# Layer norm 0 and the first projection of block 1 moved into the slots of attention layer 2

## The chip, the cores and the metric

The kernel runs on one core of one Trainium2 chip. The metric is the device time of one execution in microseconds (us): the median of three runs of the kernel before is 800.58 us (800.31 to 802.76). The engines are called by their short names: PE is TensorE (matmuls; PEld is its weight load), DVE is VectorE, ACT is ScalarE, POOL is GpSimd, and SP is SyncE, which here issues all DMAs.

## The reference

`x` is 2048 x 256, `adj` is a 2048 x 2048 matrix of zeros and ones, everything in float32. Four blocks follow one another, each with a residual and a layer norm:

```python
def _gat_layer(x, W, adj):                  # block 0: two such layers
    Wh, Ws = jnp.split(x @ W, 2, axis=-1)
    a = jax.nn.softmax(Wh @ Ws.T, axis=-1) * adj
    return jax.nn.leaky_relu(a @ Wh + x, 0.01)

x = layernorm(x + gat(gat(x)))                                          # layer norm 0
# block 1: A_ = adj + I, d = rsqrt(A_.sum(1))
x = layernorm(x + relu((A_ * d[:, None] * d[None, :]) @ x @ W))
# block 2
x = layernorm(x + relu(adj @ x / (adj.sum(1) + 1e-5) @ Wn.T + bn + x @ Ws.T + bs))
# block 3
x = layernorm(x + adj @ (relu(adj @ (x @ W1) + b1) @ W2) + b2)
```

## The kernel before

The rows are cut into 16 row tiles of 128 (`NT = 16`), and 2048 columns into 4 chunks of 512 (`NCH = 4`). A float32 product is made from high and low halves: `exact3` runs three matmuls for each 128 rows of the contraction (high by high, low by high, high by low). Every engine has its own program, written out by hand, and waits on semaphores; `ge(engine, signal, count)` is such a wait.

**Attention layers** (`layer`, l = 0 and 1, called layers 1 and 2 here). A layer first projects all rows, and then goes through 16 slots, one row tile each; `slot(b, u)` handles tile t = b + u. Slots 4 and on stand in a hardware loop. In its slot PE computes the four chunks of scores of tile t (`score`, 24 matmuls of 512 columns), transposes the masked probabilities of tile t-1 (`turn`, 16 transposes), and multiplies them with the values (`attend`, 32 matmuls). In layer 1 it also transposes the finished rows of tile t-2 (`rows`, line 1783), between score chunks 2 and 3. ACT runs the exponentials (`exp`), rounds the transposed probabilities (`hi`) and scales half of the sum (`lo_half`); DVE takes the maxima (`chunk_max`, `row_max`), the low halves (`lo`), the rest of the scaling (`scaled`) and `finish` to `finish5`: leaky relu, the residual, and mean and variance of the row, for tile t-2. POOL masks with the adjacency (`mask`), adds the layer's input (`residual`) and prepares the next query (`query`). SP loads adjacency rows and, in layer 2, input rows (`load`, lines 401 and 404).

**Layer norm 0 and the projection of block 1**, a stage of its own between layer 2 and block 1. For each of the 16 tiles: DVE normalises the rows (`n_rows`, line 1327) into one of four buffers `nrow`, SP stores them (`store0`, line 443, queue order t = 0 to 15), PE transposes them (line 1871) into one bank, ACT and DVE take high and low halves (`n_hi`, `n_lo`), PE projects them with `w1` (`n_proj`, six matmuls of 256 columns), ACT and DVE scale and split the result into `pm` (`n_moving`). The square roots of all variances are taken in two pieces (`n_deviation`, line 851), after the last exponential; the square root of the degrees (`dsq`, line 875) as well.

**Block 1** (the path taken with 0/1 adjacency is `exact`; `general` is the other one, and the choice is made by a flag that each engine reads into a register: `If(low > 0): general() Else: exact()`). SP reads each adjacency tile from HBM as bfloat16, transposed on the way (`turn_halves`, line 439; a ring of 4 buffers `at16`), POOL widens it into `adjr` (`widen`, line 664), and PE sums over it (`main_sum`, chunks c = 0 to 3, four matmuls of 512 columns each), then transposes the finished rows (`rows`, line 1944) and projects them for block 2 (`project`). The order on SP around the stage is:

```python
for t in range(RING):            # RING = 4; each waits for the end of all attention sums
    turn_halves(t)
...                              # store0 of tiles 0 to 15, then wait until all are stored
# in exact():
for t in range(RING, 2 * RING):
    turn_halves(t)
# then bout, bhid, and per slot: load_res (line 474), turn_halves(slot + 8)
```

`load_res` brings back the stored rows of a tile for the residual of block 1; DVE adds them (line 1468), takes statistics, and normalises (`xs`, line 1500), and PE needs that for `rows` (line 1944). The buffers `at16` and `adjr` lie over buffers of the attention layers, so that they can be filled only when those are done with.

Of the kernel before, what the change touches and what calls it, by code (L numbers as in the profile page):

```python
# [13 lines left out]
P = 128  # L14
# [45 lines left out]
def adjacency_resnet(nc, x, adj, w_gat, w_gcn, w_neigh, b_neigh, w_self, b_self, w1, b1, w2, b2, out):  # L60
# [26 lines left out]
    with ctx:  # L87
# [24 lines left out]
        nrow = xs + zb  # L112
# [14 lines left out]
        const = sb("constants", [P, 2])  # L127
        eps, one = const[:, 0:1], const[:, 1:2]
# [23 lines left out]
        xtall_l = sb("xtall_l", [P, KT, N], F32R, gat)  # L152
        wst_h = sb("wst_h", [P, KT, N], F32R, gat)
# [4 lines left out]
        wg_h = sb("wg_h", [P, KT, 2 * D], F32R, gat)  # L158
        wg_l = sb("wg_l", [P, KT, 2 * D], F32R, gat)
        arow16 = sb("arow16", [P, N], BF16, gat)  # L160
# [21 lines left out]
        quick = ExitStack()  # L182
        adjr = sb("adjr", [P, NT, N], F32R, quick)
        at16 = [sb(f"at16_{r}", [P, NT, P], BF16, quick) for r in range(RING)]
# [108 lines left out]
        s_dinv = sem("degree_inverses")  # L293
        s_sd0 = sem("norm0_deviation")
# [3 lines left out]
        n_out = [sem(f"norm0_rows_stored_{c}") for c in range(NCH)]  # L298
# [52 lines left out]
        def attention_bank(b, u):  # L351

            return jb[1] if isinstance(b, int) and b + u == NT - 1 else ob0

# [16 lines left out]
        def _(sp):  # L371
# [13 lines left out]
            for l, g in enumerate(G):  # L385
# [38 lines left out]
                store_halves(0, 0)  # L424
                with sp.Fori(1, NT // 2) as half:
                    b = 2 * half
                    store_halves(*before(b, 0))
                    load(b, 0)
                    store_halves(b, 0)
                    load(b, 1)  # L430
                store_halves(NT - 2, 1)

            def turn_halves(t):
                sp.wait_ge(s_a16, 16 * NT)
                if t < RING:
                    ge(sp, G[-1].av, 4 * NT)
# [4 lines left out]
            def store0(t, c):  # L441
                sp.wait_ge(n_new, t + 1)
                sp.dma_start(xs_rows[t], nrow[c][:, :]).then_inc(n_out[c], 16)

            for t in range(RING):
                turn_halves(t)
            with sp.Fori(0, NT // NCH) as q:
                for c in range(NCH):
                    store0(NCH * q + c, c)
            for c in range(NCH):  # L450
                sp.wait_ge(n_out[c], 16 * NT // NCH)
# [5 lines left out]
            def stages(quick):  # L457
                for k, a in enumerate(aggs):
# [37 lines left out]
                    def slot(b, u, fin=True):  # L496
# [9 lines left out]
                        if quick and a is C and b + u + 2 * RING < NT:  # L506
                            turn_halves(b + u + 2 * RING)
# [32 lines left out]
            def general():  # L540

                for r in range(RING):
                    sp.wait_ge(s_at[r], 16)
                for c in range(NCH):
                    load_nat(0, c)
# [5 lines left out]
            def exact():  # L551
                for t in range(RING, 2 * RING):
                    turn_halves(t)
# [10 lines left out]
        def _(pool):  # L564
# [7 lines left out]
            nc.gpsimd.tensor_tensor(bsum[:, :], bsum[:, :], bs_raw, ALU.add).then_inc(s_bsum, 1)  # L572

            for l, g in enumerate(G):
# [54 lines left out]
                slot(NT - 2, 1, nxt=False)  # L629
                slot(NT, 0, main=False, nxt=False)  # L630
# [25 lines left out]
            def widen(t):  # L656
                r = t % RING
                pool.wait_ge(s_at[r], 16 * (t // RING + 1))
                if t == 0:

                    ge(pool, G[-1].av, 4 * NT)
                    ge(pool, G[-1].msk, 4 * NT)
                    ge(pool, G[-1].zx, NT)
                nc.gpsimd.tensor_copy(adjr[:, t, :], at16[r][:, :, :].rearrange("p a i -> p (a i)"))\  # L664
                    .then_inc(s_conv, 1)

# [3 lines left out]
            def exact():  # L670
                for t in range(NT):
# [11 lines left out]
        def _(act):  # L683
# [22 lines left out]
            features(1)  # L706

            def layer(l, g, previous):
# [90 lines left out]
                def slot(b, u, main=True, av=True, fin=True, last=False):  # L799

                    p = before(b, u)
                    if av:
# [23 lines left out]
                slot(0, 0, av=False, fin=False)  # L826
                slot(0, 1, fin=False)
                slot(2, 0)
                slot(2, 1)
                with act.Fori(2, NT // 2 - 1) as half:  # L830
# [18 lines left out]
            def n_deviation(first, last):  # L849
                ge(act, G[-1].mv, last)  # L850
                nc.scalar.activation(sd[:, first:last], mv[:, first:last, 1], ACT.Sqrt, bias=eps[:, :])\
                    .then_inc(s_sd0, 1)

            def n_hi(t, u):
                act.wait_ge(n_xtr, t + 1)
                ge(act, n_prj, t - 1)
                copy(xt_h[u][:, :, :], xb[u][:, 0:D].rearrange("p (k i) -> p k i", k=KT)).then_inc(n_xth, 1)

            def n_moving(t, u):
                act.wait_ge(n_prj, t + 1)  # L860
                if not isinstance(t, int):
                    alone(act, passed["scalar"])
# [1250 lines left out]
```

## Time and profile before

| | |
|---|---|
| median of 3 runs | 800.58 us |
| profiled execution, its own time | 800.49 us |
| its span, first to last instruction | 798.7 us |
| mean granted TensorE clock | 0.977 of full speed |
| PE busy | 742.2 us (93%) |
| DVE, ACT, POOL busy | 466.6, 336.8, 322.9 us |

The span is cut into stretches by what runs in them: projections and layer 1 up to about 261 us, the projections of layer 2 to 293 us, its slots to 497 us, the stage of layer norm 0 to 530.5 us, the blocks after that. Some 1.8 us of the profiled time lie outside the span. A line of the timeline gives start, duration, engine, line of the kernel, operation, output and inputs; brackets give the idle time of the engine before it and what ended it.

### The profile page before, as it was taken

The page shows a single profiled execution, that of the slowest core. Times are in us where ns is not written, and L with a number is a line of the kernel's source. Part 1 is how long each engine was busy: PE and PEld are TensorE (multiplying, and loading weights), DVE is VectorE, ACT ScalarE, POOL GpSimd, SP SyncE. Part 2 cuts the span into 40 slices and gives each one's busy share as a digit, 9 for nine tenths or more (in the row PEclk, how much of TensorE's full clock was granted, in tenths as well). Part 3 has the DMA queues.
Part 4 walks back from the last instruction along what each step waited for, and adds up shares of the span by engine and source line. Part 5 has one row for each costly group of instructions (what it writes and reads, how often), then busy time and mean ns, then how long its engine had stood idle before and what let it go on. Part 6 is the DMA issues. An engine that isn't in the chain of part 4 may idle for free.

```text
span 798.7 us, 13828 instructions
## 1 busy us (share of the span) xinstructions
PE 742.2 (93%) x4122; PEld 630.4 (79%) x4122; DVE 466.6 (58%) x1054; ACT 336.8 (42%) x803; POOL 322.9 (40%) x313
## 2 busy tenths in 40 slices
PE   6979999999999989999999999466999999999996
PEld 5868888888888878888888888355888768879895
DVE  3667777767776555555464656443555655562377
ACT  4656565656555444343434445231222423331222
POOL 1047676766665225555546463305310011112222
PEclk9999999999999999999999999788999999998998
DMA  6052424242331303131322220669642222320033
GB/s 197 1 210 82 159 80 151 85 138 98 124 113 53 118 1 113 60 119 59 118 72 105 89 89 12 161 94 176 159 112 80 66 90 83 89 70 8 1 94 105
DMA packets 67747, 76.60 MB, mean 96 GB/s; under 512 B 36848, under 2 KB 61040, under 8 KB 63600
## 3 DMA queue, kind: packets, MB, share of 16 engines
q1 hardware_dynamic: 67696, 75.97, 31.3%
q8 instruction: 26, 0.43, 0.2%
q14 instruction: 25, 0.20, 0.1%
HBM read 48.69 MB, written 18.87 MB: 85 GB/s over the span
## 4 chain that ended last, share of the span: by engine, by line
PE 67%; issue 13%; DVE 7%; SPq 4%; DMA 3%; ACT 3%; POOL 2%; DVEq 0%; POOLq 0%; ACTq 0%
PE scores L1644 32%; PE ob L1644 25%; PE tb L1758 6%; SPq L439 3%; DMA rin<-self_term_scratch 2%; ACT stationary L685 1%; DVE stationary L1075 1%; POOL prob L594 1%; PE tb L1734 1%; PE xb L1783 1%; DVE xs L1500 1%; DVE xs L1208 1%; DMA keep<-in_x 1%; POOL zb L642 1%; POOL zb L640 1%
## 5 line engine op out<-in xcount | busy, mean ns | idle before, releaser
L594 POOL TENSOR_TENSOR prob<-prob,arow 128x512 f32<-128x512 f32 x128 | 193.2, 1530 | 169.2 <-ACT prob L770 169.2
L1644 PE MATMUL ob<-val,stationary 128*128 128x512 f32 x960 | 184.6, 344 | 0.0
L1644 PEld LDWEIGHTS ob<-val,stationary 128*128 128x128 f32 x960 | 146.7, 189 | 18.8
L1075 DVE TENSOR_TENSOR stationary<-tb,stationary 128x512 fp32r<-128x512 f32 x128 | 85.8, 689 | 70.7 <-ACT stationary L685 70.6
L685 ACT ACTIVATE stationary<-tb 128x512 fp32r<-128x512 f32 x128 | 73.0, 593 | 114.4 <-PE tb L1758 114.4
L1644 PE MATMUL ob<-pm,adjr 128*128 128x512 f32 (+1 forms) x512 | 109.5, 356 | 10.3 <-issue 5.4
L1644 PE MATMUL scores<-wst_h,whs_h 128*128 128x512 f32 x256 | 104.1, 407 | 3.8 <-ACT prob L770 3.8
L1644 PE MATMUL scores<-pm,adjr 128*128 128x512 f32 (+1 forms) x512 | 104.9, 345 | 0.0
L1644 PEld LDWEIGHTS ob<-pm,adjr 128*128 128x128 f32 x512 | 82.8, 199 | 23.0 <-issue 11.9
L1145 DVE TENSOR_REDUCE row_values<-scores 128x1 f32<-128x512 f32 x128 | 86.5, 688 | 24.4 <-PE scores L1644 24.3
L1644 PE MATMUL scores<-wst_h,whs_l 128*128 128x512 f32 x256 | 100.3, 392 | 0.0
L1644 PE MATMUL scores<-wst_l,whs_h 128*128 128x512 f32 x256 | 100.1, 391 | 0.0
L770 ACT ACTIVATE prob<-scores,row_values 128x512 f32<-128x512 f32 x128 | 86.6, 689 | 5.8 <-DVE row_values L1152 5.0
L1644 PEld LDWEIGHTS scores<-pm,adjr 128*128 128x128 f32 x512 | 79.8, 192 | 9.2
L1758 PE MATMUL tb<-ident,prob 128*128 128x128 f32 x512 | 72.2, 272 | 3.1 <-POOL prob L594 3.1
L1758 PEld LDWEIGHTS tb<-ident,prob 128*128 128x128 f32 x512 | 60.9, 140 | 13.1 <-POOL prob L594 3.9
L1644 PEld LDWEIGHTS scores<-wst_h,whs_h 128*128 128x128 f32 x256 | 48.2, 188 | 13.4 <-issue 4.5
L640 POOL TENSOR_TENSOR zb<-zb,rin 128x256 f32<-128x256 f32 x16 | 11.8, 737 | 111.5 <-DVE zb L1426 111.5
L1644 PEld LDWEIGHTS scores<-wst_h,whs_l 128*128 128x128 f32 x256 | 48.0, 188 | 10.5
L664 POOL CAST adjr<-at 128x2048 fp32r<-128x2048 bf16 x16 | 30.3, 1903 | 60.4 <-DMA at<-adjacency_halves 60.4
L1644 PEld LDWEIGHTS scores<-wst_l,whs_h 128*128 128x128 f32 x256 | 48.3, 189 | 7.5
L1185 DVE SCALAR_TENSOR_TENSOR arow<-arow 128x2048 bf16<-128x2048 f32 x16 | 43.7, 2731 | 5.0 <-issue 3.0
(160 smaller groups left out, 987.3 us busy)
## 6 DMA issues: line engine op xcount, KB each, us to landing
arow<-in_adj SPq DMA_DIRECT2D x32, 1024.0 KB, 5.2
adjacency_halves<-arow SPq DMA_DIRECT2D x16, 512.0 KB, 3.0
xres<-features_scratch SPq DMA_DIRECT2D x48, 128.0 KB, 2.1
features_scratch<-xs SPq DMA_DIRECT2D x40, 128.0 KB, 1.7
keep<-in_x SPq DMA_DIRECT2D x4, 512.0 KB, 7.0
xres<-in_x SPq DMA_DIRECT2D x16, 128.0 KB, 2.1
self_term_scratch<-rst SPq DMA_DIRECT2D x16, 128.0 KB, 1.7
rin<-self_term_scratch SPq DMA_DIRECT2D x16, 128.0 KB, 2.1
```

Of the source, the lines that this page charges most:

```text
L439: sp.dma_start_transpose(at16[t % RING][:, :, :], a16_rows[t]).then_inc(s_at[t % RING], 16)
L594: nc.gpsimd.tensor_tensor(prob[u][:, cs], prob[u][:, cs], arow[u][:, cs], ALU.mult).then_inc(g.msk.sem, 1)
L640: nc.gpsimd.tensor_tensor(zb[u][:, :], zb[u][:, :], rin[u][:, :], ALU.add).then_inc(a.rb.sem, 1)
L642: nc.gpsimd.tensor_tensor(zb[u][:, 0:HID], zb[u][:, 0:HID], bhid[:, :], ALU.add).then_inc(a.rb.sem, 1)
L664: nc.gpsimd.tensor_copy(adjr[:, t, :], at16[r][:, :, :].rearrange("p a i -> p (a i)"))\
L685: return nc.scalar.activation(dst, src, ACT.Copy, **kw)
L770: nc.scalar.activation(prob[u][:, cs], scores[:, cs], ACT.Exp, bias=nmax[u][:, :], accum_out=rs[u][:, c:c + 1]).then_inc(g.ex.sem, 1)
L1075: return nc.vector.tensor_tensor(dst, v, h.bitcast(F32), ALU.subtract)
L1145: nc.vector.reduce_max(mx[u][:, c:c + 1], scores[:, c * CH:(c + 1) * CH], AX.X)\
L1185: nc.vector.scalar_tensor_tensor(arow16[:, :], arow[u][:, :], 1.0, arow16[:, :], ALU.mult, ALU.not_equal, accum_out=bits[:, bass.ds(t, 1)])\
L1644: return nc.tensor.matmul(o, l, r, start=start, stop=stop)
L1758: last = nc.tensor.transpose(tb[c % 2][:, q * P:(q + 1) * P], prob[u][:, j * P:(j + 1) * P], ident[:, :])
```

## The change

What it does:

- `n_rows`, `n_hi`, `n_lo`, `n_proj`, `n_moving` of tiles 0 to 11 run inside slots 4 to 15 of layer 2 (slot t handles tile t-4), those of tiles 12 to 14 among the last attention sums, tile 15's after them. Only the two `xs` buffers are used. One bank, `xb0`, takes the transposes and the projection (halves of it); the last four tiles alternate with a second one.
- `n_deviation` runs for two tiles at the end of each odd slot of layer 2 on ACT, ahead of `lo_half`, and is followed by an exponential of a constant (`spent`), which brings the exponential's table back.
- `dsq`, `rdeg`, `dinv` are computed at the start of layer 2's slots.
- In both layers PE's `rows` comes after score chunk 3, no longer before it, and DVE's `rows_lo` after `row_max`.
- SP issues `turn_halves` 0 to 2 early in layer 2, 3 after its scores, and only 4 and 5 in `exact()` (before: 0 to 3 after the attention, 4 to 7 in `exact()`). `store0(t)` follows `load(t + 4)` in the loop.
- POOL widens tiles 0 and 1 before the last `residual`, 2 and on after the branch.
- PE computes tiles 0 and 1 of block 1 side by side, chunk by chunk, with tile 15's `n_rows` and `n_proj` among them.
- On PE the condition is turned round: `If(low < 1): exact() Else: general()`.

```diff
-        nrow = xs + zb
 # sync
+            load(2, 0)
+            for t in range(RING - 1):
+                turn_halves(t)
+            load(2, 1)
+            with sp.Fori(2, NT // 2) as half:
+                b = 2 * half
+                for u in range(2):
+                    load(b, u)
+                    store0(b + u - 4, u)
+            turn_halves(RING - 1)
+            for t in range(NT - 4, NT):
+                store0(t, t % 2)
...
             def exact():
-                for t in range(RING, 2 * RING):
+                for t in range(RING, RING + 2):
                     turn_halves(t)
 # gpsimd
                 slot(NT - 2, 1, nxt=False)
+                if l == LAYERS - 1:
+                    widen(0)
+                    widen(1)
                 slot(NT, 0, main=False, nxt=False)
...
             def exact():
-                for t in range(NT):
+                for t in range(2, NT):
                     widen(t)
 # scalar, slot()
                     if fin:
                         rows_hi(*before(b, u, 2))
+                    if norm:
+                        n_hi(b + u - 4, u)
...
                         exp(b, u, 3)
+                    if norm:
+                        n_moving(b + u - 4, u)
+                    if u and fin and l == LAYERS - 1:
+                        n_deviation(b - 2)
+                        n_deviation(b - 1)
+                        if not last:
+                            nc.scalar.activation(spent[:, :], one[:, :], ACT.Exp).then_inc(s_spent, 1)
...
                 cast_halves(0, 0)
+                if l == LAYERS - 1:
+                    act.wait_ge(s_cst, 2)
+                    ge(act, G[0].deg, NT)
+                    nc.scalar.activation(dsq[:, :], deg[:, :], ACT.Sqrt, bias=one[:, :]).then_inc(s_dsq, 1)
 # vector, slot()
+                    if turned:
+                        n_inverse(b + u - 4)
                     if main:
                         chunk_max(b, u, 1)
+                    if turned:
+                        n_rows(b + u - 4, u)
                     if norm:
                         finish2(*pp)
...
                         row_max(b, u)
+                    if fin:
+                        rows_lo(*pp)
+                    if turned:
+                        n_lo(b + u - 4, u)
...
                         row_sum(*p)
+                    if turned:
+                        n_moving(b + u - 4, u)
 # tensor, slot()
                         score(b, u, 1)
                         score(b, u, 2)
+                        score(b, u, NCH - 1)
                     if fin:
                         rows(*before(b, u, 2))
-                    if main:
-                        score(b, u, NCH - 1)
+                    if norm and l == LAYERS - 1:
+                        n_rows(b + u - 4, u)
...
                         attend(*p, 1)
+                        if norm and l == LAYERS - 1:
+                            n_proj(b + u - 4, u)
 # tensor, after layer 2
             turn(NT - 2, 1, 2)
+            n_rows(NT - 4, 0)
             attend(NT - 2, 1, 0)
             turn(NT - 2, 1, 3)
             attend(NT - 2, 1, 1)
+            n_proj(NT - 4, 0)
+            n_rows(NT - 3, 1)
             attend(NT - 2, 1, 2)
+            n_proj(NT - 3, 1)
+            n_rows(NT - 2, 0)
             attend(NT - 2, 1, 3)
+            n_proj(NT - 2, 0)
 # tensor, exact()
+                main_sum(0, 0, 0, 0)
+                main_sum(0, 0, 1, 0, signals=0)
+                main_sum(0, 0, 0, 1)
+                main_sum(0, 0, 1, 1, signals=0)
+                n_rows(NT - 1, 1)
+                main_sum(0, 0, 0, 2)
+                main_sum(0, 0, 1, 2, signals=0)
+                n_proj(NT - 1, 1)
+                main_sum(0, 0, 0, NCH - 1)
+                main_sum(0, 0, 1, NCH - 1, signals=NCH)
...
-                    slot(2, 0, fin=not k, late=k > 0)
-                    slot(2, 1, fin=not k, late=k > 0)
+                    slot(2, 0, fin=False, late=True)
+                    slot(2, 1, fin=False, late=True)
...
-            with pe.If(low > 0):
-                general()
-            with pe.Else():
-                exact()
+            with pe.If(low < 1):
+                exact()
+            with pe.Else():
+                general()
```

`late=True` means that `rows` of tile 0 comes after the last chunk of tile 2, `project` of tile 0 after the first chunk of tile 3, and `rows` of tile 1 after its second.

## Rows read from the trace of the kernel before

**Rows 1.** Busy time by stretch: PE, PEld, DVE, ACT, POOL, granted clock, DMA share, GB/s.
```profile
496.80:511.00 14.20, 3.56 (x25) 2.67 (x22) 5.76 (x14) 3.01 (x8) 8.24 (x5) 0.81 0.83 186
530.50:545.80 15.30, 9.88 (x36) 8.02 (x36) 0.97 (x2) 0.95 (x2) 4.94 (x3) 0.78 1.12 144
545.80:553.20 7.40, 0.89 (x4) 0.38 (x3) 3.26 (x6) 0.66 (x2) 4.48 (x3) 0.78 0.88 176
```

**Rows 2.** Waits of PE from 496 to 640 us: total, times, longest.
```profile
PE xb L1871 <- DVE xs L1327: 9.7, 1, 9.7
PE xb L1944 <- DVE xs L1500: 6.6, 1, 6.6
PE ob L1644 <- issue: 5.4, 1, 5.4
```

**Rows 3.** Timeline of PE, layer 1 (rows) and layer 2 (first matmul of two slots).
```profile
69.29 0.44 PE L1783 MATMUL xb<-ident,xs 128*128 128x128 f32 x2
...
164.00 0.44 PE L1783 MATMUL xb<-ident,xs 128*128 128x128 f32 x2 [0.17 <-DVE xs L1208]
...
231.54 0.44 PE L1783 MATMUL xb<-ident,xs 128*128 128x128 f32 x2
...
308.57 0.40 PE L1644 MATMUL scores<-wst_h,whs_h 128*128 128x512 f32 x1
...
321.43 0.40 PE L1644 MATMUL scores<-wst_h,whs_h 128*128 128x512 f32 x1
```

**Rows 4.** The chain that ended last, in order of time: a transposed and a projected tile.
```profile
519.56 0.22 PE scores L1871 x2
519.78 0.83 PE scores L1644 x6
```

**Rows 5.** Timeline of ACT: the end of a slot, and its change of table.
```profile
475.95 0.48 ACT L685 ACTIVATE tmp<-ob,row_values 128x256 f32<-128x256 f32 x1 [1.65 <-PE ob L1644]
...
490.17 1.28 ACT L875 ACT_TABLE_LOAD   x1
491.46 0.31 ACT L875 ACTIVATE dsq<-deg,constants 128x16 f32<-128x16 f32 x1
```

**Rows 6.** Start of layer 2's slots, timelines of ACT and PE.
```profile
293.94 0.69 ACT L770 ACTIVATE prob<-scores,row_values 128x512 f32<-128x512 f32 x1 [4.20 <-DVE row_values L1152]
...
294.86 0.47 PE L1644 MATMUL scores<-wst_h,whs_h 128*128 128x512 f32 x1 [1.88 <-ACT prob L770]
```

**Rows 7.** Timeline, the last tile: last sum, scaling, deviation, and the last normalised rows.
```profile
495.16 1.66 PE L1644 MATMUL scores<-val,stationary 128*128 128x512 f32 x8
497.37 0.48 DVE L1194 SCALAR_TENSOR_TENSOR zb<-scores,row_values,tmp 128x256 f32<-128x256 f32 x1 [1.01 <-ACT tmp L685]
501.39 0.29 ACT L851 ACTIVATE sd<-mv,constants 128x2 f32<-128x2 f32 x1 [1.34 <-DVE mv L1235]
526.81 0.41 DVE L1327 TENSOR_SCALAR zb<-keep,mv,rstd 128x256 f32<-128x256 f32 x1
```

**Rows 8.** Timeline of DVE, POOL and PE: the first rows of block 1.
```profile
551.14 2.05 DVE L1500 TENSOR_SCALAR xs<-zb,mv,rstd 128x256 f32<-128x256 f32 x1
551.15 1.89 POOL L664 CAST adjr<-at 128x2048 fp32r<-128x2048 bf16 x1 [2.76 <-DMA at<-adjacency_halves]
...
553.24 0.69 PE L1944 MATMUL xb<-ident,xs 128*128 128x128 f32 x2 [6.55 <-DVE xs L1500]
...
560.47 0.38 PE L1944 MATMUL scores<-ident,xs 128*128 128x128 f32 x2
```

**Rows 9.** Timeline of SP's DMA issues around the stage.
```profile
496.92 9.52 SPq L439 DMA_TRANSPOSE at<-adjacency_halves  x4
...
530.33 13.94 SPq L439 DMA_TRANSPOSE at<-adjacency_halves  x4
544.32 0.57 SPq L465 DMA_DIRECT2D bout<-in_L_gnn_b  x1
...
545.42 0.43 SPq L474 DMA_DIRECT2D xres<-features_scratch  x1
```

**Rows 10.** Timeline of PE, its last matmul.
```profile
793.33 0.41 PE L1644 MATMUL scores<-w3bh,xt_l 128*128 128x256 f32 x1
```

More of the change, by code:

```diff
@@ L847, in _ @@
             _, hi, lo_half = last_layer
[L849 to L862, printed above, removed]
-                copy(pm[:, t, 0:D], jb[u][:, 0:D], scale=dinv[:, bass.ds(t, 1)]).then_inc(n_ph, 1)
             def keep_adj(t, c):
@@ L870, in keep_adj @@
                 copy(adjt[:, t, c * CH:(c + 1) * CH], tb[c % 2][:, :]).then_inc(C.kept.sem, 1)
[L873 to L875 removed]
             hi(NT - 2, 1, 2)
[L877 removed]
+            n_hi(NT - 4, 0)
             hi(NT - 2, 1, 3)
[L879 to L896 removed]
+            n_moving(NT - 4, 0)
+            n_hi(NT - 3, 1)
+            n_deviation(NT - 2)
+            n_moving(NT - 3, 1)
+            n_hi(NT - 2, 0)
+            n_moving(NT - 2, 0)
+            lo_half(NT - 2, 1)
+            n_deviation(NT - 1)
+            n_hi(NT - 1, 1)
             n_moving(NT - 1, 1)
@@ L1020, in slot @@
                             keep_proj(*pp)
-                    if k == 0:
-                        slot(0, 0, ep=False, fin=False)
-                        slot(0, 1, fin=False)
-                    else:
-                        lo_half(0, 0)
-                        if a is not F:
-                            deviation(0, 0)
+                    lo_half(0, 0)
+                    if a is not F:
+                        deviation(0, 0)
                     slot(2, 0)
@@ L1371, in _ @@
-            n_lo(2, 0)
             finish3(NT - 2, 1)
-            n_moving(1, 1)
             finish4(NT - 2, 1)
             finish5(NT - 2, 1)
-            def n_step(q, c, ahead=True):
-                n_lo(NCH * q + c - 1, 1 - c % 2)
-                if ahead:
-                    n_rows(NCH * q + c + 1, (c + 1) % NCH)
-                n_moving(NCH * q + c - 2, c % 2)
-            n_rows(NCH, 0)
-            with dve.Fori(1, AHEAD - 1) as q:
-                for c in range(NCH):
-                    n_step(q, c)
@@ L1387, in _ @@
-            n_inverse(NT - 2, NT, 2)
-            for c in range(NCH):
-                n_step(AHEAD - 1, c, ahead=c < NCH - 1)
+            n_inverse(NT - 1)
+            n_rows(NT - 1, 1)
             n_lo(NT - 1, 1)
-            n_moving(NT - 2, 0)
             n_moving(NT - 1, 1)
@@ L1680, in _, with n_rows, n_proj @@
             features(1)
+            def n_rows(t, u):
+                pe.wait_ge(n_new, t + 1)
+                ge(pe, n_xtl, t)
+                for k in range(KT):
+                    last = nc.tensor.transpose(n_banks(t)[0][:, k * P:(k + 1) * P], xs[u][:, k * P:(k + 1) * P],
+                                               ident[:, :])
+                last.then_inc(n_xtr, 1)
+            def n_proj(t, u):
+                pe.wait_ge(n_xtl, t + 1)
+                ge(pe, n_pl, t)
+                exact3(n_banks(t)[1], [(xt_h[u][:, k, :], xt_l[u][:, k, :], w1h[:, k, :], w1l[:, k, :])
+                                       for k in range(KT)]).then_inc(n_prj, 1)
             def layer(l, g, previous):
```

297 lines of the change are left out of this document (137 added, 160 removed).

## The prediction

> **What bounds the kernel now.** I read the busy time by stretch first. In the attention slots PE is busy throughout at full clock, so what is added to PE there lengthens them. Between the attention and the middle of block 1 that breaks down: PE is busy 3.56 of 14.20 us after the last attention sum, 9.88 of 15.30 before block 1's first finished rows, 0.89 of 7.40 before its first transposes, and the granted clock is 0.78 to 0.81, between the two levels of 1.2 and 2.4 GHz [rows 1]. The waits of PE name the holes: 9.7 us for normalised rows (they wait for stores, which stand behind four transposing DMAs on SP), 6.6 us for block 1's first rows, and 5.4 us of "issue" at the branch into `exact()` [rows 2]. PE has nothing to overlap there. The third thing to see is small and repeated: in layer 1 PE's `rows` waits for DVE. From 69.29 to 231.54 us lie 12 slots of 13.52 us, while a slot of layer 2, which has no such step, takes 321.43 - 308.57 = 12.86 [rows 3].
>
> **The change, part by part.** I sum against the profiled execution (800.49 us; the median of the runs is 800.58, the same). Positions below are on the clock of the trace before; what the change adds or saves ahead of them comes into the sum at the end.
>
> *Layer 1, `rows` behind chunk 3.* Of the 0.66 us by which its slot is longer, the two transposes are 0.22 [rows 4], the rest, 0.44, is the wait for `xs` and its restart. With chunk 3 (six matmuls of 512 columns, 1.4 us) ahead, the wait has cover. ACT's and DVE's parts for these rows move behind `row_max`, where DVE would wait anyway. 14 slots x 0.44 = 6.2; the first and last wait less, so I take **5.5 saved**, bounds 0 (another link of the same ring PE, ACT, DVE takes over) and 6.2.
>
> *Start of layer 2.* ACT gets a square root between two table loads: 2 x 1.28 + 0.31 = 2.9 us [rows 5]. It has been idle for 4.20 us before its first exponential [rows 6], so this fits, if the second load stands ahead of the wait for the row maximum; behind it, 1.3 us go on the path, since PE already waits 1.88 us for that exponential [rows 6]. DVE's two reciprocals and its wait for `dsq` delay the first maximum a little. I take **0.4 lost**, bounds 0 and 1.6.
>
> *Slots 4 to 15.* PE gets two transposes and six matmuls of 256 columns: 0.22 + 0.83 = 1.05 us [rows 4]; without the first matmul's extra 0.1 us, 0.9. Twelve tiles: **12.6 lost**, bounds 10.8 and 12.8. The other engines: DVE gets some 1.5 us a slot (four operations like those of 0.41 and 0.48 [rows 7]) and stays near 9 of 13.9. ACT is the tight one. In an odd slot it has 1.65 us idle before `lo_half` [rows 5], plus the 1.05 by which the slot grows, 2.7 in all. It gets `n_moving` 0.48, two roots of 0.29 [rows 7], two loads of 1.28 and a one-column exponential of about 0.2: 3.8. So `lo_half` is 1.1 us late. Late next: `scaled` on DVE, behind it `chunk_max`, `lo`, `finish` and `n_rows` of the next tile. PE asks for these rows 6.5 us into the slot; DVE, 0.3 us late after absorbing the rest in its own waits, has them at about 5.8. Cost 0, with 0.7 us of slack. The table load itself is 1.28 us in the row, and the next ACTIVATE starts 0.01 us after it [rows 5]. The Trainium skill, "ScalarE: Activation LUTs", What ACT_TABLE_LOAD costs, adds a drain of about 1380 ns to every switch, 2.66 us together, and asks for roots and exponentials in batches, which speaks against this change; the row shows no such drain, and a rival below follows the rule. SP's `store0` ahead of the next `load` holds it until DVE's `n_rows`; an adjacency row is used a whole slot later, so 0. Three transposing DMAs at its start hold `load(2, 1)` for some 7 to 11 us, which the same slot covers.
>
> *Tail of the attention.* The last sum ended at 495.16 + 1.66 = 496.8 [rows 7]. Now tiles 12 and 13 and the transposes of 14 stand before it (2 x 1.05 + 0.22 = 2.3). Some waits come: the first `hi` of tile 15 is behind roots and a table load, and `n_rows(12)` behind `hi` and `lo`: 1.0. And POOL widens tiles 0 and 1 while DVE normalises: DVE's `xs` of 0.41 us [rows 7] took 2.05 when a cast of 1.89 started with it [rows 8]. By that row a collision costs 0 to 1.9 us, two casts up to 3.8; I take 1.2. The sum ends at 501.3. The skill, "SBUF — State Buffer", Who interferes with whom, states that DVE and POOL share a port pair as an exclusive lock for operations with two SBUF inputs or in a two-port mode; the rows agree.
>
> *Tile 15.* After the last sum come `n_proj(14)` 0.83, ACT's `n_moving` 0.48 ahead of `lo_half`, 0.15 of handing over, then as before 1.03 to the end of `scaled` [rows 7]: 503.8. From there to its deviation it was 501.68 - 497.85 = 3.8 us [rows 7], of which about 0.8 was other tiles' work: 506.8. Inverse and `n_rows`: 507.4; a collision with `widen(2)`, `widen(3)`, 1.2 (0 to 3.8): **508.6**.
>
> *SP.* From the end of the last `n_rows` to the first transposing DMA in `exact()` went 530.33 - 527.22 = 3.1 us [rows 7, 9]: 511.7. Then two such DMAs, no longer four. Four took 9.52 us after the attention and 13.94 in `exact()` [rows 9]; two cost 4.8 to 7.0, I take 6.5, since the second case is this place. 1.15 us later (bias loads) the first `xres` is issued [rows 9], at 519.4; from there to PE's first `rows` of block 1 it was 553.24 - 545.42 = 7.8 us [rows 8, 9], or 6.2 if no cast holds DVE. So `rows(0)` comes at **527.2**.
>
> *PE meanwhile.* From 501.3: `n_proj(14)` 0.8, a branch, tiles 0 to 2 at about 3.9 us each with a wait of 2 us for tile 15's rows. It reaches `rows(0)` at about 518 with a branch of 1 us, 522 with one of 5.4. Either is before 527.2. So **turning the condition round is worth nothing**; it is covered by SP's chain. A stall of 6.6 us comes back as one of about 9, clock drop included. At the kernel's end PE now jumps over `general()`: 793.74 + 5.4 = 799.1 [rows 2, 10] against a span of 798.7, at most 0.4; I take 0.
>
> *Where block 1 stands.* Before, `rows(1)` came at 560.47 [rows 8], with tiles 0 to 2 and one chunk of tile 3 done. Now it comes with one chunk more (four matmuls of 512 columns, twice the 0.12 us of 256 [rows 4], 0.9). After `rows(0)` PE has 4.1 us of work, before it took 7.2 [rows 8]; DVE's seven operations for tile 1 are the longer chain, about 5.4. So 527.2 + 5.4 = 532.6 against 560.5 + 0.9 = 561.4: **28.8 saved**. Later tiles of the adjacency come five slots ahead, so nothing more.
>
> Sum: 28.8 - 12.6 + 5.5 - 0.4 = 21.3; 800.5 - 21.3 = **779**.
>
> **Rivals.**
> - *Everything in block 1's start goes well*: no collisions (2.4 less), transposing DMAs at 2.4 us (1.7 less), no cast over the first rows (1.6 less). For it: casts are short and the earlier four DMAs ran so. 773.5. Chance 0.15.
> - *Layer 1 gives nothing*: DVE's ring (hi, lo, finish) takes the wait over. For it: the wait is there in slot after slot, so two rings are close; against: 1.4 us of new cover. 784.5. Chance 0.12.
> - *Each switch on ACT costs 1.4 us more*, as a drain would: `lo_half` is 3.9 us late in 7 odd slots, DVE's rows for the next slot 2.8 late less 0.7 slack, 2.1 x 6 = 12 or so: 791. Against it, [rows 5]. It is the skill's rule named above. Chance 0.05.
> - *Slower*: the same place, n_rows of the next slot behind a late `lo_half`. It decides from 22 us / 6 = 3.6 us of stall a pair of slots, which is 3.6 + 0.7 of lateness beyond mine, a switch of about 3.4 us. No row shows one. 803 or more. Chance 0.03.
> - *The change doesn't do what it says*: `rows(0)` does not come earlier, because SP's transposes or POOL's casts of tiles 2 to 4 are late by 20 us; PE then only holds the work in other places. 798 to 802. Against: two DMAs instead of four. Chance 0.02.
>
> The forecast itself has 0.63, with its own range 775 to 784. The range for 8 in 10 takes in the first two rivals and part of the bounds (the two collisions at 3.8 each would give 784; with layer 1 at half its gain, 787; all of the first rival with tiles at 0.9 us, 771): 770 to 788. A measurement here tells 0.3%, 2.4 us. Faster 0.94, same 0.02, slower 0.04.
>
> **What the profile after would show.** Right: slots of layer 1 of about 13.1 us with no wait of PE for `xs`; slots of layer 2 from the fourth on of 13.9 us with PE busy throughout; 16 table loads of 1.28 us; no hole of 9.7 us; a hole of 7 to 11 us before the first transposes of block 1, ended by `xs`, which waited for `xres`. Wrong: slots of layer 2 above 14.2 us in pairs (ACT's switches), PE waiting for `xs` in layer 1 still, or the hole gone (then SP's chain is shorter than I made it, and the time is near 770).

## The result, and the profile after

The changed kernel takes 778.84 us in the median of four runs (775.42 to 782.98), the kernel before 801.31 beside it (800.31 to 802.76): a ratio of 0.973, 95% interval 0.969 to 0.977. The forecast was 779. The profiled execution took 778.11 us, its span is 776.3.

The two profiles can't be compared position by position, because executions differ by up to 3.7 us at the start, in work that the change doesn't touch. A matmul of 512 columns goes from 0.63 to 0.39 us at 16.6 us here and at 13.8 in the profile before, and from 54 to 58 us this execution ran at a granted clock of 0.57. So PE began the slot with the first `rows` at 66.82 us, 2.85 later than before; a second execution of the same kernel had no such shift (its first `rows` of layer 1 stands at 70.25 us, here it is 73.17). Positions below are compared after the shift, or by distances inside one run.

The busy time by stretch of the changed kernel (PE, PEld, DVE, ACT, POOL, granted clock, DMA share, GB/s): a slot of layer 1, two slots of layer 2, the tail of the attention, tile 15, tiles 2 and 3 of block 1 [rows 1].

```profile
86.30:99.40 13.10, 13.10 (x76) 11.31 (x75) 9.90 (x17) 7.86 (x18) 9.22 (x8) 1.00 0.35 122
462.00:490.00 28.00, 28.00 (x168) 24.42 (x165) 17.50 (x44) 15.78 (x36) 12.71 (x12) 1.00 0.28 96
490.00:512.00 22.00, 19.36 (x123) 16.52 (x122) 14.66 (x35) 11.89 (x28) 9.74 (x7) 1.00 0.20 53
512.00:530.00 18.00, 10.25 (x39) 7.68 (x38) 6.04 (x11) 1.63 (x4) 6.72 (x4) 0.87 0.49 66
530.00:536.00 6.00, 5.87 (x21) 4.25 (x20) 2.19 (x6) 1.04 (x3) 2.63 (x2) 0.81 1.24 222
536.00:545.00 9.00, 8.53 (x39) 6.51 (x39) 6.47 (x16) 2.73 (x8) 4.99 (x3) 1.00 0.84 207
```

PE has no idle time in either kind of slot; the weak stretch is now 18 us long. PE's timeline, `rows` of layer 1, `n_rows` of two slots of layer 2, then `n_rows` of tile 15, tile 2's sum, and `rows` of tiles 0 and 1 of block 1 [rows 3, 8]:

```profile
73.17 0.38 PE L1811 MATMUL xb<-ident,xs 128*128 128x128 f32 x2
...
86.24 0.38 PE L1811 MATMUL xb<-ident,xs 128*128 128x128 f32 x2
...
475.63 0.38 PE L1700 MATMUL xb<-ident,xs 128*128 128x128 f32 x2
...
489.43 0.38 PE L1700 MATMUL xb<-ident,xs 128*128 128x128 f32 x2
...
518.78 0.69 PE L1700 MATMUL scores<-ident,xs 128*128 128x128 f32 x2 [4.11 <-DVE xs L1129]
519.12 2.05 PE L1658 MATMUL ob<-pm,adjr 128*128 128x512 f32 x4
...
529.49 5.25 PE L1658 MATMUL ob<-pm,adjr 128*128 128x512 f32 x16 [3.24 <-DVE zb L1443]
...
535.11 0.44 PE L1947 MATMUL xb<-ident,xs 128*128 128x128 f32 x2
...
539.52 0.44 PE L1947 MATMUL scores<-ident,xs 128*128 128x128 f32 x2 [0.47 <-DVE xs L1516]
```

A slot of layer 1 is 86.24 - 73.17 = 13.07 us (before 13.52), one of layer 2 13.80 (12.86). The holes of 9.7, 6.6 and 5.4 us [rows 2] are gone, and two others stand there: 4.11 us for tile 15's normalised rows, 3.24 us for the bank in which DVE's `total` (line 1443) still has tile 0's sum. What held that `total` shows in the timelines of ACT, POOL and DVE:

```profile
527.34 0.47 ACT L706 ACTIVATE tmp<-ob,dinv 128x256 f32<-128x256 f32 x1 [3.54 <-issue]
...
513.65 4.08 POOL L600 CAST adjr<-at 128x2048 fp32r<-128x2048 bf16 x2 [0.16 <-POOL zb L630]
...
513.98 2.00 DVE L1270 TENSOR_TENSOR keep<-keep,xres 128x256 f32<-128x256 f32 x1
...
516.97 0.79 DVE L1290 COPY mv<-norm_values 128x2 f32<-128x2 f32 x1
...
523.84 0.48 DVE L1142 SCALAR_TENSOR_TENSOR pm<-scores,dinv,pm 128x256 fp32r<-128x256 f32 x1 [3.49 <-ACT pm L706]
528.96 0.48 DVE L1443 SCALAR_TENSOR_TENSOR zb<-ob,dinv,tmp 128x256 f32<-128x256 f32 x1 [4.63 <-issue]
532.67 0.61 DVE L1484 SCALAR_TENSOR_TENSOR zb<-zb,xres 128x256 f32<-128x256 f32 x1 [3.23 <-DMA xres<-features_scratch]
...
534.64 0.41 DVE L1516 TENSOR_SCALAR xs<-zb,mv,rstd 128x256 f32<-128x256 f32 x1
```

"issue" is a wait for nothing that the profile shows: here ACT and DVE jump over `general()` into `exact()`, 3.54 and 4.63 us, behind their last instruction for tile 15 and therefore in the open (that it is the jump, the run with the early branch shows below). And DVE's operations at 513.98 and 516.97 took 2.00 and 0.79 us while POOL's casts of tiles 2 and 3 ran. SP's queue [rows 9]:

```profile
521.62 4.50 SPq L447 DMA_TRANSPOSE at<-adjacency_halves  x2
526.17 0.57 SPq L480 DMA_DIRECT2D bout<-in_L_gnn_b  x1
...
527.26 0.43 SPq L489 DMA_DIRECT2D xres<-features_scratch  x1
```

`xres` landed at 532.57, 5.31 us after its issue (2.1 in the median of such loads), `xs` was ready at 535.05, and PE had come to `rows(0)` at 534.98. Two chains end together there: SP's and the one through the branches.

### The profile page after: what moved, and what is told of

It reads as the page before. It is cut to its first block, busy times and chain, and to the rows that moved or that the text cites. A ratio compares the mean times of both kernels' runs of the same rounds, so it can differ in the third digit from the quotient of the medians.

```text
span 776.3 us, 13790 instructions
## 1 busy us (share of the span) xinstructions
PE 734.9 (95%) x4122; PEld 628.3 (81%) x4122; DVE 474.8 (61%) x1068; ACT 356.5 (46%) x837; POOL 323.3 (42%) x313
## 4 chain that ended last, share of the span: by engine, by line
PE 74%; issue 9%; DVE 6%; DMA 4%; ACT 2%; POOL 2%; SPq 2%; POOLq 0%; DVEq 0%; ACTq 0%
PE scores L1658 36%; PE ob L1658 27%; PE tb L1786 7%; DMA rin<-self_term_scratch 2%; PE xb L1658 1%; DMA xres<-features_scratch 1%; POOL prob L623 1%; PE tb L1762 1%; DVE xs L1516 1%; DVE zb L1484 1%; POOL zb L674 1%; POOL zb L672 1%; DMA keep<-in_x 1%; SPq L447 1%; DVE norm_values L1490 1%
## 5 line engine op out<-in xcount | busy, mean ns | idle before, releaser
L1658 PE MATMUL ob<-val,stationary 128*128 128x512 f32 x960 | 186.7, 344 | 0.0
L1658 PE MATMUL ob<-pm,adjr 128*128 128x512 f32 (+1 forms) x512 | 106.9, 349 | 8.8 <-DVE pm L1095 4.2
L1658 PEld LDWEIGHTS ob<-pm,adjr 128*128 128x128 f32 x512 | 80.1, 192 | 21.5 <-issue 5.9
```

The costliest lines, as they stand in the source:

```text
L1658: return nc.tensor.matmul(o, l, r, start=start, stop=stop)
```

## The experiments

All are measured beside the kernel before, which took 800.51 to 802.54 us in the median of its runs there; ratios are to it and compare better than medians. Since starts differ, the table compares positions after `n_rows` of tile 12 (489.43 above, called the mark), in the one profiled execution of each: PE's `n_rows(15)`, `rows(0)` and `rows(3)` of block 1.

```
kernel                    n_rows(15)  rows(0)  rows(3)   median   ratio
changed                      29.35     45.68    60.33    778.84   0.973 (0.969 to 0.977)
the same again               29.32     46.98    60.89    779.01   0.974 (0.970 to 0.977)
PE's condition as before     29.41     45.69    60.90    775.84   0.971 (0.969 to 0.973)
early branch                 29.31     46.56    61.92    778.69   0.971 (0.968 to 0.973)
input tiles first            30.04     47.43    61.65    780.97   0.974 (0.972 to 0.975)
both                         29.31     40.87    62.87    779.26   0.971 (0.969 to 0.974)
casts 2, 3 late              27.15     44.34    59.56    777.09   0.969 (0.967 to 0.972)
both, transposes late        29.32     41.69    56.40    772.32   0.965 (0.962 to 0.968)
  + casts 2, 3 late          27.13     38.67    53.73    771.28   0.962 (0.959 to 0.965)
  + casts 0, 1 late          26.28     37.85    51.76    769.32   0.963 (0.960 to 0.967)
```

**`rows` behind chunk 3, alone.** The kernel before with only this part of the change, in both layers (on DVE `rows_lo` moves behind `row_max` as well).

```diff
                         score(b, u, 2)
+                        score(b, u, NCH - 1)
                     if fin:
                         rows(*before(b, u, 2))
-                    if main:
-                        score(b, u, NCH - 1)
```

> The kernel before with one part of the change alone: in both attention layers PE's rows comes after score chunk 3, and DVE's rows_lo after row_max. Theory: layer 1's slots go from 13.5 us to 13.07 us, as in the trace of the changed kernel, because PE no longer waits for xs; 14 slots give 6.1 us, so about 795 us, ratio to before 0.992. Rival (the gain of layer 1 belongs to the other edits, or DVE's ring takes the wait over): slots stay at 13.5 us and the time at 801 us.

796.33 us, ratio 0.995 (0.993 to 0.997). PE's timeline of it:

```profile
70.42 0.38 PE L1783 MATMUL xb<-ident,xs 128*128 128x128 f32 x2
...
83.50 0.38 PE L1783 MATMUL xb<-ident,xs 128*128 128x128 f32 x2
```

A slot takes 13.08 us, as in the changed kernel, while the waits of the stage behind the attention stand about as before (10.0, 6.6 and 4.8 us). So the shorter slots are this edit's, and no other ring takes the wait over. By the slots it is worth 6.1 us, and the two profiled executions differ by 6.7; the medians differ by 4.3 only (2.5 to 5.7 by the interval of the ratio), and where the rest goes wasn't found.

**PE's condition turned back.** The changed kernel with `If(low > 0): general() Else: exact()` on PE.

> The changed kernel with PE's condition turned back, so that PE jumps over the general path again. Theory: the branch costs PE about 5.4 us again, as before; 4.1 us of that is covered by the wait for tile 15's normalised rows, which stays, and what is left over is below 1.5 us: 779 to 780.5 us. PE's first sum of block 1 begins 5 us later, the transposes of tile 15 at most 1.5 us later. Rival (falling through is a main part of the gain): 783 to 784 us, all 5.4 us on the path.

Its idle times in PE's timeline:

```profile
510.98 1.15 PE L1658 MATMUL ob<-pm,adjr 128*128 128x512 f32 x4 [3.16 <-issue]
...
514.12 0.97 PE L1658 MATMUL ob<-pm,adjr 128*128 128x512 f32 x3 [0.86 <-issue]
...
525.76 5.53 PE L1658 MATMUL ob<-pm,adjr 128*128 128x512 f32 x16 [3.98 <-DVE zb L1443]
...
532.13 0.44 PE L1947 MATMUL xb<-ident,xs 128*128 128x128 f32 x2 [0.60 <-DVE xs L1516]
```

The jump costs 3.16 us and another 0.86, and takes them out of the wait for tile 15, which is gone. `rows(0)` comes 45.69 us after the mark, not 45.68. The time, 775.84 us, is 3 us below the 779 to 780.5 expected and below the changed kernel's, but the intervals of the ratios overlap (0.969 to 0.973, 0.969 to 0.977). Falling through is worth nothing here.

**No table loads in the slots.** The changed kernel with ACT copying the variance where it took its root; the root is left out.

```diff
-                nc.scalar.activation(sd[:, bass.ds(t, 1)], mv[:, t, 1:2], ACT.Sqrt, bias=eps[:, :]).then_inc(s_sd0, 1)
+                nc.scalar.activation(sd[:, bass.ds(t, 1)], mv[:, t, 1:2], ACT.Copy).then_inc(s_sd0, 1)
```

> The changed kernel with layer norm 0's square roots replaced by a copy of the variance (so its rows are not normalised by the deviation), which leaves the number of operations and takes out the 13 table loads in the slots. Theory: the loads are hidden, PE's slots stay at 13.8 us, and the time stays within 1 us of 778.8. Rival (each pair of loads delays PE by way of lo_half and the next tile's normalised rows): slots shorter by 0.3 us or more, 3 us or more in all.

777.91 us, ratio 0.972 (0.969 to 0.975); `n_rows` in the slots comes every 13.79 us, the same. The switches are hidden. In the changed kernel ACT's odd slot reads:

```profile
467.60 1.28 ACT L731 ACT_TABLE_LOAD   x1
468.89 0.48 ACT L731 ACTIVATE sd<-mv,constants  x2
469.39 1.28 ACT L862 ACT_TABLE_LOAD   x1
470.68 0.20 ACT L862 ACTIVATE constants<-constants 128x1 f32<-128x1 f32 x1
470.79 0.46 ACT L706 ACTIVATE tmp<-ob,row_values 128x256 f32<-128x256 f32 x1
```

467.60 + 1.28 = 468.88, and the root begins at 468.89: no drain between a load and what follows it. Nor is there one ahead of a load: the roots end at 469.37, and the second load begins at 469.39. The Trainium skill, "ScalarE: Activation LUTs", What ACT_TABLE_LOAD costs, states 1283 ns for the load, which the row matches, and about 1380 ns of drain for every switch, of which these rows show nothing.

**A second pair of switches.** Six odd slots of the changed kernel get a root and an exponential of a constant more.

```diff
     nc.scalar.activation(spent[:, :], one[:, :], ACT.Exp).then_inc(s_spent, 1)
+    nc.scalar.activation(again[:, :], one[:, :], ACT.Sqrt).then_inc(s_spent, 1)
+    nc.scalar.activation(back[:, :], one[:, :], ACT.Exp).then_inc(s_spent, 1)
```

> The changed kernel with a second root and a second exponential of a constant behind spent, in 6 odd slots: two more table loads of 1.28 us and two short operations, 3.0 us more of ACT ahead of lo_half. Theory: in the changed kernel the normalised rows of an even slot are ready 0.35 us before PE asks for them, so 2.6 us of the 3.0 come out as PE's wait for xs in each even slot after, about 15 us in all: 794 us. Rival (there is more slack than that, since DVE waits elsewhere): under 6 us.

801.71 us, ratio 1.001 (0.998 to 1.005), not the 794 expected: 3.0 us more on ACT in six places, and the change's whole gain is gone. PE's `n_rows`, and what stands behind it, after three of the six waits:

```profile
405.98 0.43 PE L1703 MATMUL xb<-ident,xs 128*128 128x128 f32 x2 [2.66 <-DVE xs L1132]
...
406.60 1.64 PE L1661 MATMUL ob<-val,stationary 128*128 128x512 f32 x8
...
466.87 0.69 PE L1703 MATMUL xb<-ident,xs 128*128 128x128 f32 x2 [2.65 <-DVE xs L1132]
467.35 1.06 PE L1789 MATMUL tb<-ident,prob 128*128 128x128 f32 x4
468.06 2.40 PE L1661 MATMUL ob<-val,stationary 128*128 128x512 f32 x8
...
498.57 0.44 PE L1703 MATMUL xb<-ident,xs 128*128 128x128 f32 x2 [2.57 <-DVE xs L1132]
```

The waits came as expected (2.57 to 2.92 us, 16.0 in six). But the last of these `n_rows` comes 23.7 us later than in the changed kernel: 498.57 - 475.63 = 22.9, and 0.8 more by the shift at the start. A pair of slots, 27.6 us in the changed kernel, grew by 5.6, 4.4, 2.9, 2.9 and 4.1 us from one wait to the next; the last is 498.57 - 466.87 - 27.6. Where a pair grew by more than its wait, matmuls are slow behind the wait: behind 466.87 the transposes took 1.06 us in place of 0.60 and eight matmuls 2.40 in place of 1.64, at a granted clock of 0.66 (467 to 471 us), behind the first wait 0.50 (341 to 346 us). Behind 405.98 the clock stayed at 1.00 and next to nothing was lost. Over the six a wait of PE cost about half as much again, which my 15 us left out; why some cost it and others don't stays open.

**The two chains at `rows(0)`.** First, ACT's and DVE's last instructions of tile 15 ahead of the flag are written into both bodies. So ACT jumps before it waits for tile 15 at all, and DVE, which still normalises tile 15 ahead of its jump, before it waits for tile 15's projection. On ACT `last_tile()` is the three calls taken away, and it stands in `general()` too; on DVE it is `n_moving` alone.

```diff
-            n_deviation(NT - 1)
-            n_hi(NT - 1, 1)
-            n_moving(NT - 1, 1)
...
             def exact():
+                last_tile()
```

> The changed kernel with the last instructions of tile 15 that stand ahead of the If on ACT (its deviation, its halves and its copy for the transposes) and on DVE (its copy for the transposes) written into both bodies instead, so that ACT and DVE take their branch before they wait for tile 15. In the changed kernel ACT's first lo_half behind its branch began 3.54 us and DVE's first total 4.63 us after the last work ahead of it, with nothing else in the way, and TensorE waited 3.24 us for that total's bank; but the xs of block 1 was ready at 535.05, where TensorE reached rows(0) at 534.98. Theory A (two chains end there together, SP's of the transposing DMAs and the input tile, and TensorE's through the branches of ACT and DVE): the wait of 3.24 us on the total goes, TensorE comes to rows(0) some 3 us sooner and waits there 3 us for xs; the time stays within 0.3% of the changed kernel's, 777 to 779. Theory B (the branches alone set rows(0)): 775, 0.4% less. Theory C (code of ACT's branch fetched again at each place): slower by 1 to 2 us.

Then SP's first two input tiles ahead of the transposing DMAs.

```diff
             def exact():
+                for u in range(2):
+                    sp.dma_start(xres[u][:, :], xs_rows[u]).then_inc(C.xres[u].sem, 16)
                 for t in range(RING, RING + 2):
                     turn_halves(t)
```

> The changed kernel with SP issuing the input tiles of block 1's first two row tiles ahead of the two transposing DMAs of the last halves, behind which they stood. In the changed kernel the first of them was issued at 527.26, landed 5.31 us later, and xs was ready at 535.05. Theory A (two chains): xs is ready some 3 us sooner or more, but TensorE still comes to rows(0) at about 535, held by the bank that DVE's total of tile 0 gives back after its branch: 777 to 779. Theory B (SP's queue alone sets rows(0)): 774 to 775. If the transposing DMAs, now later by the issue of two loads (about 1.2 us), are needed sooner than I think, 780.

Then both.

> Both edits at once: the branches of ACT and DVE taken ahead of tile 15, and SP's two input tiles ahead of the transposing DMAs. If two chains of equal length end at rows(0), only this one gains: the wait of 3.24 us on the total goes and no wait for xs takes its place, 774 to 775.5 (3 to 4 us under the changed kernel). If only one of the two sets it, this run equals the better of the other two. If neither does, 778.

With the early branch alone (778.69 us, theory A), `total` comes 1.43 us behind ACT and not 4.63 behind "issue"; PE's wait for the bank is gone, and all of it, and more, comes back as a wait for `xs`, in the timelines of DVE and PE:

```profile
522.82 0.48 DVE L1446 SCALAR_TENSOR_TENSOR zb<-ob,dinv,tmp 128x256 f32<-128x256 f32 x1 [1.43 <-ACT tmp L706]
...
533.02 0.69 PE L1952 MATMUL xb<-ident,xs 128*128 128x128 f32 x2 [5.49 <-DVE xs L1519]
```

With the input tiles alone the wait for the bank stays (3.77 us). Its time, 780.97, is above theory A's 777 to 779, but its ratio, 0.974, is the changed kernel's. The third theory, 780 for transposed tiles that come too late, has the time and a `rows(3)` 0.8 to 1.3 us later for it, and against it that PE waits for no cast; it is not excluded. Either leaves `rows(0)` at 46.6 to 47.4 after the mark; both bring it to 40.87, without a wait. So there were two chains of one length, as theory A had it. But the time, 779.26, has nothing of these 5 us. PE's timeline of the run with both:

```profile
541.64 0.69 PE L1954 MATMUL xb<-ident,xs 128*128 128x128 f32 x2 [4.19 <-DVE xs L1521]
541.98 3.76 PE L1665 MATMUL ob<-pm,adjr 128*128 128x512 f32 x8
545.54 0.63 PE L1665 MATMUL scores<-w2h,xt_h 128*128 128x512 f32 x1
```

That is `rows(2)`: its input tile was issued at 534.04, behind four transposing DMAs (6.12 us for two, 5.86 for two), a third chain. The 8.4 us from 541.6 run at a granted clock of 0.65, between the levels of 1.2 and 2.4 GHz, and eight matmuls take 3.76 us where they take 2.10. At `rows(3)` the run is 2.0 to 2.5 us behind the two executions of the changed kernel. My 774 to 775.5 was wrong for want of that queue.

**Casts of tiles 2 and 3 late.** POOL waits for tile 15's normalised rows. (The "weight chunk" in the text on record is the adjacency of tiles 2 and 3.)

```diff
                 if t == 2:
+                    pool.wait_ge(n_new, NT)
```

> The changed kernel with POOL's cast of the weight chunk that ran from 513.65 for 4.08 us (two casts) made to wait until DVE has normalised tile 15. Beside those casts DVE's keep of tile 15 took 2.00 us and its copy of the moments 0.79, where the same operations took 0.42 and 0.17 elsewhere. Theory A (both hold the same port and tile 15's chain sets everything behind it): n_rows of tile 15 and all that follows come 2.2 us sooner, 776 to 777. Theory B (something else of the chain, SP's queue or the branches, has that much slack): 778. If the chunk is then late for block 1's first matmuls, it costs up to 4 us: 780 to 782, and the wait on it stands in the profile.

`n_rows(15)` comes 2.2 us sooner, the (2.00 - 0.43) + (0.79 - 0.17) of the two slowed operations. Of these 1.3 us are left at `rows(0)` and 0.8 at `rows(3)` against the first execution of the changed kernel, 2.6 and 1.3 against the second; the ratio, 0.969, can't be told from the changed kernel's. PE's rows:

```profile
516.95 0.44 PE L1701 MATMUL scores<-ident,xs 128*128 128x128 f32 x2 [1.94 <-DVE xs L1130]
517.14 1.17 PE L1659 MATMUL ob<-pm,adjr 128*128 128x512 f32 x4
```

Four matmuls take 1.17 us behind a wait of 1.94 us, and 2.05 in the changed kernel behind one of 4.11. It is not the length of the wait alone: in the last two runs below the same four took 1.81 and 1.72 us behind 1.93 and 1.91. The Trainium skill, "SBUF — State Buffer", Who interferes with whom, says that DVE and POOL lock a shared port pair against each other; this run agrees, since moving the casts alone brought DVE's 2.00 us down to 0.43.

**All chains shortened.** The changed kernel once more, as the reference of the three others; then both edits with the transposing DMA of tile t + 4 in slot t, not that of t + 6; then the late casts of tiles 2 and 3 added; then those of tiles 0 and 1, behind tile 13's rows.

```diff
-                        if quick and a is C and b + u + RING + 2 < NT:
-                            turn_halves(b + u + RING + 2)
+                        if quick and a is C and 2 <= b + u < NT - RING:
+                            turn_halves(b + u + RING)
...
                 if t == 0:
+                    pool.wait_ge(n_new, NT - 2)
```

> The changed kernel itself once more, on the chip and in the rounds of the three that follow, so that these are compared with it and not with its other runs. From the end of layer 2's last attention sum it comes to rows(0) 25.1 us later and to rows(3) 29.7 + 5 us, that is 39.7 us later, and its last matmul ends 259.4 us later.

> The branches of ACT and DVE taken ahead of tile 15 and SP's first two input tiles ahead of the transposing DMAs, as in the run with both, and now also the transposing DMA of tile t + 4 issued in slot t of block 1 in place of that of tile t + 6. With both edits TensorE came to rows(0) 20.27 us after the last attention sum in place of 25.06, but waited 4.19 us at rows(2) for an xs whose input tile SP issued behind four transposing DMAs (12.0 us in its queue), ran the 8.3 us behind that wait at 0.63 us for a matmul that takes 0.40 elsewhere, and had lost all again at rows(3): 42.3 us after the last sum against 39.7. Theory A (SP's queue is the third chain): now only two of the four stand ahead of tile 2's input tile, rows(2) waits less than 1 us, rows(3) comes 35.5 us after the last sum, 4 us under the changed kernel: 774 to 775. Theory B (the casts of POOL need the transposed tiles early): a wait on adjr or on the casts at tiles 4 to 6 takes its place, and the time stays at 778.

> The same with POOL's cast of tile 2 and those behind it made to wait until DVE has normalised tile 15, which alone brought tile 15's n_rows 2.2 us and rows(2) 0.8 us nearer to the last attention sum. If the chains are now short enough, its full 2.2 us come through: rows(3) some 33.5 us after the last sum, 6 us under the changed kernel, 771 to 773. If the casts, which now begin behind tile 15, meet DVE's work on tiles 0 and 1 instead, half of it is given back.

> The same with the casts of tiles 0 and 1 waiting for tile 13's normalised rows as well, so that they leave the last slots of the attention alone, where they slowed DVE's xs to 0.95, keep to 1.51 and the next xs to 1.98 us and TensorE waited 1.32 and 0.6 us. Worth up to 1 us: 770 to 772. If those casts then run into tile 15's chain, it is worth nothing or costs 1 us.

Unchanged, 779.01 us. It comes to `rows(0)` 26.4 us after the last attention sum, not 25.1, and to `rows(3)` 40.3, not 39.7 (the 29.7 in the text on record is a slip), so a position scatters by about 1.3 us, and differences below that are not to be read. With the third chain cut, 772.32 (774 to 775 expected); no wait for a cast or a transposed tile takes its place, and `rows(2)` waits 0.36 us. The transposing DMAs late without the two other edits were not tried; that all three are needed is argued from the waits, not shown. The casts, worth 0.8 or 1.3 us at `rows(3)` alone, are worth 2.7 there now, from one execution each. Together 769.32, some 9 us under the changed kernel at `rows(3)` and in the median (ratio to before 0.963, interval 0.960 to 0.967, against 0.970 to 0.977), the lowest median found. Up to `rows(3)` PE's idle times behind layer 2's slots are all of these, with the four matmuls behind the longest:

```profile
496.27 0.63 PE L1795 MATMUL tb<-ident,prob 128*128 128x128 f32 x4 [0.32 <-DVE stationary L1103]
...
498.22 0.44 PE L1709 MATMUL xb<-ident,xs 128*128 128x128 f32 x2 [1.32 <-DVE xs L1137]
...
504.65 0.36 PE L1667 MATMUL scores<-w1h,xt_h 128*128 128x256 f32 x1 [0.42 <-DVE pm L1150]
...
513.76 0.44 PE L1709 MATMUL scores<-ident,xs 128*128 128x128 f32 x2 [1.91 <-DVE xs L1137]
513.96 1.72 PE L1667 MATMUL ob<-pm,adjr 128*128 128x512 f32 x4
...
519.42 0.50 PE L1667 MATMUL ob<-pm,adjr 128*128 128x512 f32 x1 [0.39 <-DVE pm L1150]
```

The last two versions, 771.28 and 769.32, can't be told apart: the ratios are 0.962 and 0.963 with overlapping intervals, and the 2.0 us between them at `rows(3)` come from one execution each.

## Why the prediction was right

The sum held; one step of the account behind it, what PE does meanwhile, did not.

- *Layer 1*, 5.5 saved: 6.1 in the profile (the distance to the profile before, +2.85 us at the first `rows`, was -3.29 at the end of the layer). Shown by the first experiment; the rival that it gives nothing falls.
- *Start of layer 2*, 0.4 lost: PE waits 2.15 us where it waited 1.88 [rows 6], 0.3. The second table load ran at 288.00, ahead of the wait for the row maximum, and ACT was still idle for 1.55 us.
- *Slots 4 to 15*, 12.6 lost: (475.63 - 461.84) - 12.86 = 0.93 a tile, 11.2. The extra 0.1 us of a first matmul is not paid inside a busy stream, the lower bound of my row. DVE had the next tile's rows ready at 475.30, 0.33 us before PE asked, where I reckoned 0.7. The rivals of ACT's switches fall with that row, but the point from which they decide was too far off: I asked for 4.3 us of lateness more to lose everything, and 3.0 were enough, because slow matmuls came behind three of the six stalls.
- *Tail*: with the shift at this place, 11.2 - 6.1 + 0.3 + 2.85 = 8.25 us, the last sum ended at 510.05 - 8.25 = 501.8, predicted 501.3. I had 2.2 us for waits and the collision together; PE waited 2.6 in four places (0.33, 1.32, 0.57, 0.42).
- *Tile 15*, 508.6: PE's `n_rows` at 518.78 - 8.25 = 510.5. The mis-sized term is the collision, 2.2 us for my 1.2.
- *SP*: 2.9 us to the first transposing DMA (3.1), 4.50 for two (6.5), 1.14 to `xres` (1.15), 7.85 to `rows(0)` (7.8). These 4.50 us are the shortest of this place in the twelve profiles that have it (4.50 to 6.21; 4.99 in the second execution), so their size is partly luck. The 2 us that the DMAs were shorter make up for tile 15, and `rows(0)` is at 535.11 - 8.25 = 526.9, predicted 527.2.
- *PE meanwhile*: here the account failed. I had PE at `rows(0)` by 518 to 522 with a hole of about 9 us there. It came at 534.98 - 8.25 = 526.7 and did not wait. That is one of my signs of being wrong, the hole gone, though not for the reason that I gave with it: SP's chain was only 2 us shorter, the rest is PE coming 5 to 9 us later. I had looked at PE's branch and left out ACT's and DVE's, 3.54 and 4.63 us, and the bank that tile 2 needs back from `total(0)`; and the slow matmuls behind each of the two waits (2.05 us for four; 5.25 for 16, against 3.93 in the run with the early branch). Both chains happen to end within 0.1 us of each other. That is luck, and by it the time of `rows(0)` was right and the place of the hole was not. That turning the condition is worth nothing held, but not because of SP's chain alone.
- *Block 1*, 28.8 saved: `rows(1)` at 539.52 - 8.25 = 531.3 against 561.4, 30.1; it came 4.4 us behind `rows(0)`, not 5.4. How much of the 30.1 belongs to the norm in the slots, to the early transposing DMAs or to tiles 0 and 1 side by side, no run separates.

The sum by measured terms: 30.1 - 11.2 + 6.1 - 0.3 = 24.7 saved, less 2.85 by the slower start of this execution, 21.9; the spans differ by 22.4. The second execution of the changed kernel, which began without that shift, bears the 24.7 out: its span is 773.8 us, 24.9 below the kernel before. The forecast of 21.3 was thus 3.4 us short of what the change itself gives in these profiles, and in the first of them the chance of the start brought it back. The medians differ by 22.5 and, in the second set, 21.5 us; in how many of their executions the start was late, no profile tells.

## What to carry to other kernels

When a stage is folded into the slots of another, look at every engine's branch and queue behind the last step, not at PE's alone: here three chains (the branches of ACT and DVE, the input tile behind transposing DMAs, the input tile of tile 2 behind four of them) ended within a few us of each other, and neither of the first two fixes, nor both together, showed in the time until the third chain was cut. So compare the position of a named instruction from run to run, and try the fixes together before dropping them. Slack on an engine off the path is worth measuring by doubling its load: 3.0 us more on ACT in six places cost this change's whole gain.

## What of the hardware was not expected

- A wait of TensorE can be paid again behind it, in slow matmuls, and the length of the wait doesn't settle whether. Waits of 2.57 to 2.92 us in the slots made a pair of slots 2.9 to 5.6 us longer. Behind 1.91 to 1.94 us four matmuls took 1.17, 1.72 or 1.81 us, behind 4.11 us 2.05; after a wait of 4.19 us the granted clock was 0.65 over 8.4 us. Behind the 1.32 us in the tail eight matmuls took 1.66 us in nine of the ten executions of the table, and 2.89 in the one with the input tiles first.
- A branch over a body that isn't run cost 3.54 us on ACT, 4.63 on DVE and 3.16 + 0.86 on PE. It is not a constant: in the other runs with this order ACT's took up to 4.25 us and DVE's up to 6.10. It can be hidden by placing it where the engine is idle anyway.
- The two transposing DMAs at the start of `exact()` held SP for 4.50 and 4.99 us in two executions of the same kernel, and for up to 6.21 in the other versions. What decides it stays open; it wasn't tried.
